# A decoder layer on one core: experts reordered, their weights loaded in two parts, both shared experts begun on the first half of the tokens

## What is computed

```python
logits = hidden @ gate_weight.T; scores = sigmoid(logits)        # 16 routed experts
# 2 of 4 groups, then the top 4 experts; weights normalised, times 2.5
topk_weight, topk_idx = _route(hidden, gate_weight, bias)
_swiglu(x, gw, uw, dw) = silu(x @ gw.T) * (x @ uw.T) @ dw.T      # F = 128 per expert
# sum over routed experts of weight * swiglu, plus a shared swiglu with F = 256
```

## Time and profile before

| | |
|---|---|
| three timed runs | 601.23, 598.18, 596.38 us; median 598.18 us |
| the profiled execution's own time | 597.41 us |
| its span, first to last instruction | 595.5 us |
| mean granted clock of PE | 0.991 of full |
| busy: PE, DVE, ACT, POOL | 557.4, 437.1, 398.3, 298.9 us |
| part that the change touches | from about 393 us to the end |

### The profile page before, as it was taken

The page is one execution under the profiler, slowest core; times in us unless marked ns, Lnnn a source line. Parts: engine busy times, 40 slices in busy tenths (PEclk is TensorE's granted clock), DMA queues, the critical chain, the costliest instruction groups (busy, mean ns, idle before and its releaser), DMA issues.

```text
span 595.5 us, 10331 instructions
## 1 busy us (share of the span) xinstructions
PE 557.4 (94%) x3392; PEld 488.2 (82%) x3392; DVE 437.1 (73%) x1046; ACT 398.3 (67%) x783; POOL 298.9 (50%) x201
## 2 busy tenths in 40 slices
PE   3899999999999999999999999897777799999996
PEld 1687889989989989989989988786566688888885
DVE  8778989989989988998998998968593433333334
ACT  4978988878978979879779778665531433343331
POOL 2434756746746646656666563301041655556542
PEclk9998999999999999999999999999998899999999
DMA  6122032032032032032031020110002433333311
GB/s 206 29 107 81 0 117 81 1 116 81 2 117 81 2 116 81 2 116 75 8 116 56 27 97 23 59 29 1 0 1 70 149 105 107 104 123 113 108 62 70
DMA packets 16267, 42.23 MB, mean 71 GB/s; under 512 B 4544, under 2 KB 4800, under 8 KB 16224
## 3 DMA queue, kind: packets, MB, share of 16 engines
q1 hardware_dynamic: 16224, 41.69, 20.9%
HBM read 40.47 MB, written 1.21 MB: 70 GB/s over the span
## 4 chain that ended last, share of the span: by engine, by line
PE 83%; DVE 8%; ACT 4%; DMA 2%; issue 2%; SPq 1%; ACTq 0%; DVEq 0%
PE bank L1258 20%; PE bank L1260 19%; PE bank L1259 19%; PE bank L1254 15%; PE bank L1396 5%; PE bank L1384 4%; ACT tok L624 2%; DMA xbias<-in_xb 1%; DMA w_raw<-in_w 1%; DVE stats L976 1%; DVE xT_lo L911 1%; DVE gated_lo L1158 1%; ACT values L538 0%; DVE x L1248 0%; DVE raw L995 0%
## 5 line engine op out<-in xcount | busy, mean ns | idle before, releaser
L1258 PE MATMUL bank<-xT_lo,w_hi 128*128 128x512 f32 x336 | 140.0, 417 | 3.6 <-DVE conv L1149 1.3
L1260 PE MATMUL bank<-xT_hi,w_hi 128*128 128x512 f32 x336 | 132.3, 394 | 0.0
L1259 PE MATMUL bank<-xT_hi,w_lo 128*128 128x512 f32 x336 | 131.8, 392 | 0.0
L425 POOL TENSOR_TENSOR gated_lo<-gated,gated_hi 128x512 fp32r<-128x512 f32 x30 | 38.7, 1290 | 116.5 <-ACT gated_hi L644 112.8
L624 ACT ACTIVATE tok<-bank,nmr,rstd 128x128 f32<-128x128 f32 x256 | 91.0, 504 | 2.1 <-DVE nmr L891 2.1
L502 POOL TENSOR_TENSOR gate<-conv,tap 128x512 f32<-128x512 f32 x36 | 46.4, 1291 | 84.5 <-DVE conv L1149 71.4
L1258 PEld LDWEIGHTS bank<-xT_lo,w_hi 128*128 128x128 f32 x336 | 63.5, 189 | 18.8 <-DVE conv L995 3.2
L1260 PEld LDWEIGHTS bank<-xT_hi,w_hi 128*128 128x128 f32 x336 | 63.3, 188 | 14.2
L420 POOL TENSOR_TENSOR conv<-tap,conv 128x506 f32<-128x506 f32 x32 | 61.9, 1934 | 21.8 <-DVE conv L995 21.8
L420 POOL TENSOR_TENSOR raw<-tap,raw 128x506 f32<-128x506 f32 x32 | 61.9, 1934 | 20.3 <-DVE raw L995 16.3
L1259 PEld LDWEIGHTS bank<-xT_hi,w_lo 128*128 128x128 f32 x336 | 63.7, 190 | 9.6
(11 more groups left out here) (167 smaller groups left out, 1358.3 us busy)
## 6 DMA issues: line engine op xcount, KB each, us to landing
w_raw<-in_w SPq DMA_DIRECT2D x34, 384.0 KB, 4.4
obet<-obet_rows SPq DMA_DIRECT2D x16, 768.0 KB, 4.2
tap<-route_rows SPq DMA_DIRECT2D x16, 512.0 KB, 3.6
wv_raw<-in_wv SPq DMA_DIRECT2D x8, 256.0 KB, 4.8
wo_raw<-in_wo SPq DMA_DIRECT2D x8, 256.0 KB, 4.9
x<-in_x SPq DMA_DIRECT2D x2, 512.0 KB, 4.6
out_x<-x SPq DMA_DIRECT2D x4, 256.0 KB, 2.4
raw<-in_ctx SPq DMA_DIRECT2D x1, 512.0 KB, 5.4
```

Source lines behind the costliest of these rows:

```text
L425: nc.gpsimd.tensor_tensor(gated_lo[:, cc], gated[:, c * N:(c + 1) * N], gated_hi[:, cc].bitcast(F32), ALU.subtract).then_inc(gated_lo_read ...
L1258: nc.tensor.matmul(o, l_hi, r_lo, start=start, stop=False, skip_group_check=loose)
L1259: nc.tensor.matmul(o, l_lo, r_hi, start=False, stop=False, skip_group_check=loose)
L1260: return nc.tensor.matmul(o, l_hi, r_hi, start=False, stop=stop, skip_group_check=loose)
```

## The change

- **Softmax of the mixing.** The energies of sequences 2 and 3 go to banks 6 and 7 and come later in PE's list; `context_max(2)` moves on DVE behind the norm of the first half; on ACT the exponentials 4 to 7 move behind `half_out(1, 0)`. `mix(0)` writes banks 4 and 5 and waits for `p_added`, `mix(1)` is cut in two with `half_transpose(2, 0)` between, and the adding of the second half is cut in two as well (`add_stats`).
- **Shared experts.** PE makes gate and up of the first half of expert 1 and of expert 2 (in banks 6 and 7) around `half_transpose(2, 1)`, the second halves after it. Their `prod` is used directly: POOL's multiplying by ones is gone. `silu_g`, `prod`, `act_hi`, `act_lo` and `gate` have two places, by odd and even expert.
- **Experts 3 and 4** are split whole (768 columns) by ACT `early_high` and POOL `early_low`, during the mixing, into tiles of attention that are free by then (`wv_hi/lo`, `wo_hi/lo`). In ACT's list both stand between the exponentials and `context_soft(1)`.
- **Order of the loop.** PE runs `gate_up(n+2)`, then `down(n)`. POOL's step n is: wait for the route row of n, `weigh(n)` half 0, `gate_up_low(n+1)`, `weigh(n)` half 1, `down_low(n)`. ACT's step n: `gate_silu(n)`, `gate_up_high(n+1)`, `act_high(n)`, `down_high(n)`.
- **Loads in two parts.** From expert 7 on, gate and up (256 KB) and down (128 KB) are loaded by two DMAs, with waits of their own. A route row's index e in the code is expert e + 3.

```diff
@@ SP
-            for s in range(2):
-                load_route(s, s, NCH * (s + 1))
-            with sp.Fori(0, E_ROUTED // 2 - 1) as r:
-                for s in range(2):
-                    expert_split(r * 2 + (3 + s))
-                    load_expert(r * 2 + (5 + s), s)
-                    load_route(r * 2 + (2 + s), s, r * (2 * NCH) + NCH * (3 + s))
+            def load_route(e, s):
+                if not (isinstance(e, int) and e < 2):
+                    sp.wait_ge(e_weighted, e * NCH - NCH)
...
+            def load_gate_up(n, s):
+                sp.wait_ge(w_lo_ready, n + (H - 2))
...
+            def load_down(n, s):
+                sp.wait_ge(down_lo_ready, n - 6)
...
+            load_route(0, 0)
+            load_route(1, 1)
+            load_gate_up(7, 0)
+            load_route(2, 0)
+            load_down(7, 0)
+            load_gate_up(8, 1)
+            load_route(3, 1)
+            load_down(8, 1)
+            with sp.Fori(0, E_ROUTED // 2 - 3) as r:
+                for s in range(2):
+                    load_gate_up(r * 2 + (9 + s), s)
+                    load_route(r * 2 + (4 + s), s)
+                    load_down(r * 2 + (9 + s), s)
+            for s in range(2):
+                load_route(E_ROUTED - 2 + s, s)
@@ POOL
+            pool.wait_ge(x_mixed, 1)
+            early_low(3)
+            early_low(4)
+            pool.wait_ge(r_ready, 1)
+            gate_up_low(5, 0)
+            gate_up_low(6, 1)
+            def step(n, m, s, up=True, down=True):
+                pool.wait_ge(ld_route[s], n * 8 - (1 + s) * 8)
+                weigh(n, m, s, 0)
+                if up:
+                    gate_up_low(n + 1, 1 - s)
+                weigh(n, m, s, 1)
+                if down:
+                    down_low(n, s)
@@ ACT, down_high
-                act.wait_ge(ld_w[s], n * 8 + (8 * (H - 1 - s) + 16))
+                if not (isinstance(n, int) and n < 7):
+                    act.wait_ge(ld_down[s], n * 8 - (40 + 8 * s))
                 act.wait_ge(e_down, n - 2)
@@ ACT, before the second half of the softmax
-            context_exp((4, 5))
             context_att(0)
             half_norm(1, 0)
+            half_out(1, 0, xT)
+            context_exp((4, 5))
             context_exp((6, 7))
-            half_out(1, 0, xT)
+            early_high(3)
+            early_high(4)
             context_soft(1)
@@ ACT, experts
+            def step(n, m, s, up=True):
+                gate_silu(n, m)
+                if up:
+                    gate_up_high(n + 1, 1 - s)
+                act_high(n, m)
+                down_high(n, s)
@@ PE, mixing and shared experts
             half_transpose(1, 0)
-            mix(0)
+            mix(0, (0, 1))
             context_weights(1)
             half_transpose(1, 1)
-            mix(1)
+            mix(1, (2,))
+            half_transpose(2, 0)
+            mix(1, (3,))
...
-            gate_up(1, 0, True, (0,))
+            gate_up(1, 0, ((0, 0), (0, 1)))
+            gate_up(2, 1, ((0, 0),))
             half_transpose(2, 1)
+            gate_up(2, 1, ((0, 1),))
             router_logits(1)
...
@@ PE, routed experts
             pe.wait_ge(r_tr_ready, NCH)
-            gate_up(3, 0, chunks=(1,))
             gate_up(4, 1)
-            down(3, 0, False, False)
-            with pe.Fori(0, E_ROUTED // 2 - 1) as r:
+            gate_up(5, 0)
+            down(3, 3, 0)
+            gate_up(6, 1)
+            down(4, 4, 1)
+            with pe.Fori(0, E_ROUTED // 2 - 2) as r:
                 for s in range(2):
-                    gate_up(r * 2 + (5 + s), s)
-                    down(r * 2 + (4 + s), 1 - s, False, False)
-            down(E_ALL, 1, False, True)
+                    gate_up(r * 2 + (7 + s), s)
+                    down(r * 2 + (5 + s), 5 + s, s)
+            down(E_ALL - 1, E_ALL - 1, 0)
+            down(E_ALL, E_ALL, 1)
```

More of the change, by code:

```diff
@@ L229, in decoder_layer @@
         ld_w = [sem(f"ld_w{i}") for i in range(2)]
+        ld_down = [sem(f"ld_down{i}") for i in range(2)]
         ld_prm = [sem(f"ld_prm{i}") for i in range(G)]
@@ L488, in down_low @@
                 w = slice(s * 3 * D + 2 * D, (s + 1) * 3 * D)
-                pool.wait_ge(down_hi_ready, n - E_SHARED)
+                pool.wait_ge(down_hi_ready, n - 4)
                 nc.gpsimd.tensor_tensor(w_lo[:, w], w_raw[:, w], w_hi[:, w].bitcast(F32),
                                         ALU.subtract).then_inc(down_lo_ready, 1)
[L493 to L503, removed]
@@ L507, in _ @@
[L507 to L523, removed]
@@ L525, in _, with early_low, weigh @@
-            with pool.Fori(0, E_ROUTED // 2 - 1) as r:
+            def early_low(n):
+                hi, lo = early(n)
+                s = 1 - n % 2
+                pool.wait_ge(w_hi_ready, n + H)
+                nc.gpsimd.tensor_tensor(lo, w_raw[:, s * 3 * D:(s + 1) * 3 * D], hi.bitcast(F32),
+                                        ALU.subtract).then_inc(w_lo_ready, 1)
+            def weigh(n, m, s, c):
+                pool.wait_ge(u_prod, n * NCH + (c + 1 - NCH))
+                if not (isinstance(n, int) and n < 5):
+                    pool.wait_ge(e_hi, n * NCH + (c + 1 - 3 * NCH))
+                    pool.wait_ge(e_lo, n * NCH + (c + 1 - 3 * NCH))
+                nc.gpsimd.tensor_tensor(weighted(m, c), prod[:, two(m, c)],
+                                        wbc[:, s * T + c * N:s * T + (c + 1) * N],
+                                        ALU.mult).then_inc(e_weighted, 1)
@@ L799, in _, with router_scores @@
             half_out(1, 1, xT)
[L800 to L803, removed]
+            half_norm(2, 0)
+            half_out(2, 0, xT_hi)
+            gate_silu(1, 1, (0,))
+            half_norm(2, 1)
+            half_out(2, 1, xT_hi)
+            gate_silu(2, 2, (0,))
+            act_high(1, 1, (0,))
+            def router_scores(c):
                 act.wait_ge(r_full, c + 1)
@@ L1141, in u_times @@
[L1141 to L1159, removed]
+            def u_times(n, m, chunks=range(NCH)):
+                for c in chunks:
+                    dve.wait_ge(e_full, e_count(n, c) * 2)
+                    dve.wait_ge(g_silu, e_count(n, c))
+                    if not (isinstance(n, int) and n < 5):
+                        dve.wait_ge(e_weighted, n * NCH + (c + 1 - 5 * NCH))
+                    elif n > E_SHARED:
+                        dve.wait_ge(e_hi, (n - 3) * NCH + c + 1)
+                        dve.wait_ge(e_lo, (n - 3) * NCH + c + 1)
+                    nc.vector.tensor_tensor(prod[:, two(m, c)], e_bank(n, c, 1)[:, :], silu_g[:, two(m, c)],
+                                            ALU.mult).then_inc(u_prod, 1)
@@ L1620, in _ @@
-            half_transpose(2, 0)
+                hi, lo = w_hi[:, s * 3 * D:(s + 1) * 3 * D], w_lo[:, s * 3 * D:(s + 1) * 3 * D]
+                if isinstance(n, int) and n in (3, 4):
+                    hi, lo = early(n)
+                for c, j in parts:
+                    if isinstance(n, int) and n == 2:
+                        pe.wait_ge(*((x_mixed, 4) if c == 0 else (g_silu if j == 0 else u_prod, e_count(1, c))))
+                    elif not (isinstance(n, int) and n == 1):
+                        pe.wait_ge(g_silu if j == 0 else u_prod, e_count(n - 1, c))
+                    for kt in range(KT):
+                        o = j * D + kt * P
+                        ins = mm3(e_bank(n, c, j)[:, :], hi[:, o:o + P], lo[:, o:o + P],
+                                  xs_(xT_hi, kt, c * N, (c + 1) * N), xs_(xT_lo, kt, c * N, (c + 1) * N),
+                                  kt == 0, kt == KT - 1)
+                    ins.then_inc(e_full, 1)
```

259 lines of the change are left out of this document (156 added, 103 removed).

## The result

The changed kernel takes 624.99 us (median of 3 runs, 624.40 to 626.67) against 598.18 us before; the ratio is 1.045, with a 95% interval of 1.037 to 1.052. The forecast was 613 us, the range 603 to 624 us. The profiled execution took 626.67 us, its span is 624.9 us.

What follows compares the result with a forecast made beforehand. PE, busy 94% of the span, bounds the kernel before; the changed loop would set the pace: gate_up(7) at 474.6 us, eleven rounds of 10.7 us, 14.0 us of last work, 0.8 us clock, then the end: 613 us, range 603 to 624.

Steps and rivals of the forecast that it cites:

- part 3: Routed experts' loop: route row held behind down_low closes a loop of waits, 10.7 us an expert against PE's 8.28 us.
- part 2: First routed experts: from the routing weights' copy at 450.0 us to down_low(5) at 467.2 us, gate_up(7) at 474.6 us.
- three DMAs issued together, the route row last: Link of the loop: landing of down part, gate and up, and route row, 4.6 us, between 4.2 and 5.3 us.
- part 1: Front up to gate_up(4): of 14.7 us idle time and clock loss 7.4 us stay, so gate_up(4) starts 7.3 us earlier.
- late softmax: Front: context_soft(1) comes some 2.3 us later on ACT, and PE waits 1.3 us for the softmax.
- ACT's half of norm 1: Front: PE waits 1.9 us for this, which stands behind context_att in ACT's list.
- the up part of expert 1's second half: Front: PE still waits 1.3 us for it, as it stands in the middle of DVE's routing chain.
- POOL's blocking of DVE: Front: POOL's two early_low make norm 2's factors 1.9 us late on DVE; 1.4 us reaches PE.
- the cover of the second half's norm: Front: expert 2's gate and up fill PE's wait for the second half's low part, leaving near 0.
- PE stays the bound: Rival for the loop: only PE's work follows, no loop of waits, 583 us; chance 0.08.
- The clock in the loop: PE's clock may fall after waits; 1.6 us lost in a round is hidden, behind the last wait 0.8 us counts.
- The rule of the Trainium skill: Loop's landing: 2.0 us plus bytes at 436 GB/s, 4.1 us for 896 KB together, sum about 607 us.

Runs made afterwards that it cites:

- e1: Changed kernel with every route row issued one step earlier in SP's list, ahead of the wait for down_low that held it back: 581.59 us, ratio 0.972.
- e3: Kernel before, with only the route row of expert n moved behind the wait for down_low(n) and the load of expert n+2: 628.39 us, ratio 1.051.
- e5: Changed kernel with the route row first of the three issues behind the wait for down_low: 608.60 us.
- e6: e1 with the splits of experts 3 and 4 moved later, ACT's behind half_out(2, 0) and POOL's behind u_prod: 578.28 us, ratio 0.968.
- e2: Changed kernel with the route row issued second, ahead of the next gate and up load, still behind the wait for down_low: 620.64 us.

## Why the prediction was right in its cause and too small in its size

- **The loop of waits** (part 3): right. Every link has its line above, e1 takes it away by one issue and returns to 581.59 us, and e3 makes it in the kernel before.
- **The start of the loop** (part 2): the time is right, in part by luck. `down_low(5)` was forecast for 467.2 us and ended at 465.89 + 0.94 = 466.83 us. But the store of the routing weights was issued at 447.76 us, 2.2 us before the forecast copy at 450.0 us, and from there 7.6 us passed to the first weighing (455.40 us) instead of 5.9 us: 3.5 us instead of 1.9 us went by before the route rows were issued. The two errors nearly cancel. The first weighing, and `gate_up(7)`, forecast for 474.6 us:

```profile
455.40 5.95 POOL L553 TENSOR_TENSOR gate<-conv,tap 128x512 f32<-128x512 f32 x4 [8.18 <-DMA tap<-route_rows]
```

```profile
474.34 0.49 PE L1353 MATMUL bank<-xT_lo,w_hi 128*128 128x512 f32 x1 [3.62 <-POOL w_lo L530]
```

- **The term that was mis-sized** is the landing of "three DMAs issued together, the route row last". I took 4.6 us, with 5.3 us as the upper end; until POOL starts on the row it is 1.25 us for the two issues ahead and 4.32 us for the row, 5.57 us, 1.0 us more. The row's landing of 4.1 us was near the row of 768 KB that I used; what the 4.6 us leave out, and the 5.3 us count with 1.1 us, is that two issues stand ahead, which take 0.5 to 0.9 us each in the loop (477.90, 478.59, 479.44 us above). SP's answer was 0.03 to 0.17 us, 0.14 us in the mean, instead of 0.2 us. POOL and ACT took 6.13 instead of 5.9 us, as `weigh` of the second half was 1.73 us beside DVE's low part. A round is 11.84 instead of 10.7 us.
- **The sum**, against the profiled execution (626.7 us against 612.5 us of mine): 11 rounds by 11.87 us between the starts of `gate_up(7)` and `gate_up(18)` (474.34 to 604.96 us) are 130.6 us instead of 117.7, 12.9 us more; the start is 0.3 us early; the rest of PE's work 0.5 us shorter; from the last matmul to the end of the span 5.6 instead of 3.5 us, 2.1 us more. Together 14.2 us.

```profile
604.96 0.49 PE L1353 MATMUL bank<-xT_lo,w_hi 128*128 128x512 f32 x1 [1.86 <-POOL w_lo L530]
...
618.99 0.28 PE L1355 MATMUL bank<-w_hi,gated_hi 128*128 128x256 f32 x1
```

- **The front** (part 1) won more than the forecast: `gate_up(4)` starts at 448.31 us instead of 450.8 us, so that 4.9 us of the 14.7 us stayed and not 7.4 us. PE waited 0.8 us for the late softmax instead of 1.3, 1.7 us for ACT's half of norm 1 (forecast 1.9), 0.2 us for the up part of expert 1's second half (forecast 1.3), and nothing through POOL's blocking of DVE (forecast 1.4). That the cover of the second half's norm leaves near 0 is right (0.4 us for both halves). What I had not in the sum is a fall of the clock from 408 to 420 us, to 0.50 at its lowest; it cost about 1.2 us, an estimate: 4.9 us less the 3.8 us that PE was idle from 405 to 440 us. The 2.5 us won did not reach the end, because the route row and not PE set the start of the loop.

```profile
448.31 0.39 PE L1353 MATMUL bank<-xT_lo,wo_hi 128*128 128x512 f32 x1
```

- **The rival "PE stays the bound"** would have given 583 us; e1, which opens the loop, takes 581.59 us. So the rest of the sum holds to 2 us.
- **The clock in the loop** fell, as I had allowed (0.86), and was hidden by the round nearly everywhere: the two rounds in which DVE's `prod` came last took 11.70 and 11.56 us, no longer than the others.
- **The rule of the Trainium skill** that I set against the landing ("DMA: Bandwidth & Descriptors", section "Anatomy of one DMA — SWDGE (gpsimd) path") would have given an estimate of 4.1 us from the first issue to landing; the trace has 5.57 us to POOL's start. For the row alone the rule gives an estimate of 3.2 us, the trace 3.8 us when it is issued first (e5) and 3.6 us in the kernel before. The rule is for a DMA from GpSimd; these come from SP.

The range ended at 624 us, 1 us short. Its upper end had the landing at 5.3 us and so the round at 11.4 us; both were above that, 5.57 and 11.84 us.

## What to carry to other kernels

In a queue that issues in order, look at what each issue stands behind, not only at what it waits for itself. If the wait ahead of it needs the work that the issue feeds, there is a loop, and its length, not the busy time of any engine, is the time of a round. Sum it link by link, and count each issue ahead of the one that is needed as a link of its own. A load that already has a free place belongs ahead of waits for places that come free later.

## What the runs showed of the chip, unexpected

- Where PE leads, executions of one kernel differ mostly as their mean clock does: the kernel before took 594.6 us at 0.994 and 602.4 us at 0.983, e6 577.7 us at 1.000 and 580.6 us at 0.994. In the changed kernel, where the loop leads, they do not: 625.0 us at 0.981 and 624.4 us at 0.977.
- A row of 512 KB lands (median) in 3.6 us in the kernel before, where the next load follows 3 us later, in 3.8 us as the first of three loads (e5), in 4.1 us as the second (e2) or the third (changed kernel), and in 4.5 us behind a load of 384 KB (e3). But in e1 it is the third as well and lands in 3.8 us, so its place among the loads is not all that sets it.
- The store of the routing weights to DRAM, 64 KB, was followed by the next issue after 1.9 us before (455.34 to 457.28 us) and after 3.5 us in the changed kernel (447.76 to 451.22 us). No run looked for the reason.
